# A graph layer with a mixture of experts on one core: which engine does the last addition of the result

## The reference

```python
z   = layernorm(x)
agg = adj @ z + beta[:, None] * z
x   = x + (agg / (adj.sum(1) + beta)[:, None]) @ gnn_kernel + gnn_bias

z      = layernorm(x)
logits = z @ Wr + br                       # 64 experts
gates  = softmax(top_2(logits))            # two per token
y_e    = relu(z @ W1[e] + b1[e]) @ W2[e] + b2[e]
x      = x + gates[:, 0] * y_first + gates[:, 1] * y_second
```

## Time and profile before

| | us |
|---|---|
| median of three runs | 410.21 |
| lowest, highest | 409.86, 410.55 |
| profiled execution | 412.09 |
| its span, first to last instruction | 410.2 |

### The profile page before, as it was taken

How to read it: one execution, slowest core, us unless ns; L and a number is a source line. 1 busy time by engine, 2 the same in 40 slices (tenths; PEclk the granted TensorE clock), 3 DMA queues, 4 the chain that set the end, 5 groups by cost and what they waited for, 6 DMA issues and landing times.

```text
span 410.2 us, 8191 instructions
## 1 busy us (share of the span) xinstructions
PE 347.5 (85%) x1973; PEld 278.4 (68%) x1973; DVE 304.0 (74%) x886; ACT 171.1 (42%) x264; POOL 225.8 (55%) x220
## 2 busy tenths in 40 slices
PE   6989899989999999999999364598999999999200
PEld 2445786876868868688686131498999999999200
DVE  4778689889799898998988262366776767777167
ACT  3485466745855658557480310011111111112063
POOL 3450002058878668576683726075777777777600
PEclk9999899999999999999999758599999999999755
DMA  8999998998978969889680104598999999996097
GB/s 312 369 423 381 347 401 335 389 427 338 419 294 348 408 244 420 325 331 415 241 343 7 47 7 150 165 279 259 300 310 292 295 294 291 295 274 211 27 352 262
DMA packets 45623, 119.25 MB, mean 291 GB/s; under 512 B 7705, under 2 KB 19630, under 8 KB 37410
## 3 DMA queue, kind: packets, MB, share of 16 engines
q1 hardware_dynamic: 27938, 95.88, 62.7%
q10 hardware_dynamic: 12672, 14.58, 11.8%
q0 software_dynamic: 4992, 8.54, 5.7%
HBM read 104.02 MB, written 16.78 MB: 294 GB/s over the span
## 4 chain that ended last, share of the span: by engine, by line
PE 34%; DVE 30%; DMA 16%; ACT 11%; issue 4%; SPq 2%; POOL 2%; POOLq 1%; ACTq 0%; DVEq 0%
DVE adj_low L679 15%; PE bank L978 9%; DMA adj_ring<-adj_t 7%; ACT adj_high L557 6%; PE bank L988 5%; PE bank_pair L988 5%; ACT payload L572 3%; DMA x_sb<-x 3%; PE bank L972 2%; PE bank_pair L985 2%; DMA adj_ring<-dispatched_rows 2%; PE bank L985 2%; PE bank L914 2%; DVE x_sb L842 2%; DMA expert_answers<-adj_ring,ans 2%
## 5 line engine op out<-in xcount | busy, mean ns | idle before, releaser
L679 DVE TENSOR_TENSOR adj_low<-adj_ring,adj_high 128x2048 fp32r<-128x2048 f32 x51 | 116.0, 2286 | 18.5 <-ACT adj_high L557 18.2
L557 ACT CAST adj_high<-adj_ring 128x2048 fp32r<-128x2048 f32 x51 | 97.1, 1905 | 57.7 <-DMA adj_ring<-adj_t 31.9
L502 POOL DMA_INDIRECT dispatched_rows<-payload,slot x64 | 95.2, 1487 | 44.2 <-issue 17.5
L515 POOL DMA_INDIRECT expert_answers<-adj_ring,ans x92 | 90.6, 985 | 43.0 <-ACT adj_ring L610 24.4
L910 PE MATMUL bank<-adj_high,z_hi 128*128 128x512 f32 x204 | 85.0, 417 | 0.9 <-ACT adj_high L557 0.9
L911 PE MATMUL bank<-adj_high,z_lo 128*128 128x512 f32 x204 | 80.2, 393 | 0.0
L821 DVE TENSOR_SCALAR adj_ring<-bank,adj_ring 128x128 f32<-128x128 f32 x184 | 56.0, 346 | 11.9 <-PE bank L978 10.1
L978 PE MATMUL bank<-xt_sb,adj_ring 128*128 128x128 f32 x368 | 57.0, 278 | 0.0
L914 PE MATMUL bank<-adj_low,z_hi 128*128 128x512 f32 x204 | 55.0, 391 | 0.2 <-DVE adj_low L679 0.2
L900 PE MATMUL bank<-adj_ring,z_sb 128*128 128x512 f32 x104 | 48.5, 615 | 3.2 <-DVE z_sb L665 2.8
L978 PEld LDWEIGHTS bank<-xt_sb,adj_ring 128*128 128x128 f32 x368 | 49.3, 195 | 0.0
(11 more groups left out here) (125 smaller groups left out, 426.1 us busy)
## 6 DMA issues: line engine op xcount, KB each, us to landing
adj_ring<-adj_t SPq DMA_DIRECT2D x64, 1024.0 KB, 8.9
adj_ring<-w_pack SPq DMA_DIRECT2D x48, 257.5 KB
adj_ring<-w_pack ACTq DMA_DIRECT2D x44, 257.5 KB
dispatched_rows<-pad_rows SPq DMA_DIRECT2D x8, 528.0 KB, 10.6
adj_ring<-expert_answers SPq DMA_DIRECT2D x8, 512.0 KB, 6.6
adj_ring<-dispatched_rows SPq DMA_DIRECT2D x48, 66.0 KB
adj_ring<-dispatched_rows ACTq DMA_DIRECT2D x44, 66.0 KB
out<-x_sb SPq DMA_DIRECT2D x8, 256.0 KB, 4.0
```

The costliest lines, as they stand in the source:

```text
L502: pool.indirect_dma_start(rows, bass.IndirectOffsetOnAxis(ap=slot[:, b, t, k:k + 1], axis=0), payload[:, b, t, k, :], None).then_inc(scatt ...
L515: pool.indirect_dma_start(y_tok, bass.IndirectOffsetOnAxis(ap=ans[:, s:s + 1], axis=0), y_sb[:, s, :], None, bounds_check=N * K - 1, oob_i ...
L557: nc.scalar.copy(high[:, m % PARTS], adj_sb[:, slot_of(g, k)]).then_inc(hi_ready, 1)
L679: v.tensor_tensor(low[:, m % PARTS], adj_sb[:, slot_of(g, k)], high[:, m % PARTS].bitcast(F32), ALU.subtract).then_inc(lo_ready, 1)
```

## The change

The vector engine no longer does the tensor_tensor, nor does it wait for its own scalar_tensor_tensors or for `scaled`; the last scalar_tensor_tensor of a piece signals a new semaphore. The Pool, behind its loop of scatters, waits for that semaphore and for `scaled`, adds the piece of 128x512 and signals `o_ready`. Sizes, tiles, DMAs and the order of the pieces stay.

```diff
+        first_added = sem("first_added")
...
         @block.gpsimd
...
+            for c in range(OUT_STEPS):
+                tiles = slice(c * OUT_CH, (c + 1) * OUT_CH)
+                pool.wait_ge(first_added, c + 1)
+                pool.wait_ge(scaled, c + 1)
+                pool.tensor_tensor(x_sb[:, tiles, :], x_sb[:, tiles, :], y_in[:, tiles, 1, :], ALU.add).then_inc(o_ready, 1)
...
         @block.vector
...
                 for t in tiles:
                     last = v.scalar_tensor_tensor(out=x_sb[:, t, :], in0=y_in[:, t, 0, :], scalar=gates[:, t, 0:1],
                                                   in1=x_sb[:, t, :], op0=ALU.mult, op1=ALU.add)
-                own.after(last)
-                dve.wait_ge(scaled, c + 1)
-                xs = x_sb[:, tiles[0]:tiles[-1] + 1, :]
-                v.tensor_tensor(xs, xs, y_in[:, tiles[0]:tiles[-1] + 1, 1, :], ALU.add).then_inc(o_ready, 1)
+                last.then_inc(first_added, 1)
```

## The result

The changed kernel takes 418.44 us, median of five runs (417.83 to 420.19), against 410.55 us for the kernel before (five runs, 409.86 to 411.31): a ratio of 1.0195, 95% interval 1.0167 to 1.0223, or 7.9 us more. The direction was forecast; the size was not. The forecast was +2.7 us, and the result lies above the range's end of 416.3 us. The profiled execution has a span of 418.3 us, 8.1 us more than before.

A forecast was written before the change was run, and what follows sets the result against it. The vector engine was taken to bound the tail's second half at 1.77 us a piece. Alternating with the Pool at 2.07 us ends the last addition 2.7 us later: 410.21 + 2.7 = 412.9 us, range 411.0 to 416.3.

The forecast's parts named there:

- What bounds the tail: Second half of the tail: the vector engine sets the pace at 1.77 us a piece; ScalarE needs 1.28 us.
- this bound: Tail's end without exclusion: DMA throughput limits the stores, last landing 407.7 instead of 409.8, 2.0 us less, 408.2 us.
- The two engines exclude each other, and take turns: In the tail, two-input vector instructions and Pool additions block each other by turns: 2.07 us a piece; chance 0.70.
- the sum: Tail, per piece: 0.16 + 1.27 + 0.07 + 0.57 = 2.07 us instead of 1.77; last addition 2.7 us later.
- the faster rival: In the tail, no exclusion for this form: the Pool follows ScalarE at 1.28 us a piece; 408.2 us, chance 0.12.
- The rival in which the vector engine keeps its turn: In the tail, the Pool waits until the scalar_tensor_tensors end at 403.8, then adds eight pieces; 416.1 us, chance 0.10.
- the late Pool: Before the tail's additions, skipped halves cost 1.2 us each, the Pool arrives at 399; 413 to 415 us, chance 0.03.
- The last step of the sum: At the kernel's end, SyncE's last store follows the last addition as before, with 2.0 us to land.
- the bound of the one term in the sum: Tail's piece length if nothing overlaps: 1.14 + 1.27 + 0.16 = 2.57 us a piece, time 416.4 us.
- The statement that the Pool has nothing to do in the tail: Before the tail's additions, the Pool is there in time: last scatter ends at 388.13 us, skipped halves over by 390.8.

The follow-up runs named there:

- e11: Kernel before, but for the last two pieces ScalarE applies the first answer's gate and the vector engine does two tensor_tensors a piece; ratio 0.9996.
- e4: Changed kernel, but the scalar_tensor_tensor reads its first tensor from PSUM, leaving the first answer out of the result; 414.76 us, ratio 1.0082 against the kernel before.
- e8: Changed kernel, but the Pool does a memset on a dead tile in place of each addition; span 412.4 us in a single execution.
- e1: Kernel before, plus one Pool memset of 128x1, read by nothing, behind the vector engine's last addition; 417.35 us against 411.22, ratio 1.0142.
- e3: Kernel before, but the Pool waits for the last addition's semaphore and executes nothing behind it; 416.0 us, ratio 1.0104.
- e9: Changed kernel with one explicit Pool drain between its last scatter and its first addition; 413.29 us against 411.19 for the kernel before, ratio 1.0045.

## Why the prediction was right and wrong

**What bounds the tail: right.** The vector engine's 1.77 us a piece set the end. In e11's trace the last addition moved 0.9 us with the vector engine's shorter pieces. In e4's it came 12.0 us after the tail's start, the DMA engines were full until then (shares of 0.97 to 1.05), and SyncE was through after 14.6 us, 2.1 us under before, where the prediction had 2.0 for this bound.

**The two engines exclude each other, and take turns: right.** Forecast 2.07 us a piece, measured 2.06 between the Pool's additions; scalar_tensor_tensors of up to 1.39 us, the mean 562 ns ("near 0.6 us"); additions of 1.26 to 1.31 us. That the totals agree to 0.01 us is partly luck, two small errors that cancel: an addition took 1.31 us where the sum had 1.27, and the Pool stood still for 0.75 us between two of them where the sum had 0.80 (0.07 + 0.57 + 0.16). The last addition was forecast 2.7 us later and came 2.56 us later, measured from the tail's start. e4 and e8 show that this is the exclusion: take away one SBUF input or the Pool's reading, and it is gone. The narrow reading of the Trainium skill, Advanced Engine Details and Errata, section VectorE Performance Modes (the fast two-port modes alone), one of the grounds for the faster rival, does not hold here: the scalar_tensor_tensor of 0.34 us took 1.39 us. The rival in which the vector engine keeps its turn did not happen, since the Pool's additions begin at 394.23, with most of the vector instructions still to come; nor did the late Pool, which stood idle 6.68 us before its first addition.

**The last step of the sum failed.** It said: "SyncE's last store follows as before, with 2.0 us to land". The store did follow as before, with 2.0 us. What failed is what was left unsaid, that the store still ends the program. The program ends when the last engine has drained, and the Pool's drain costs 8.2 us, hidden in the kernel before because the Pool's last instruction ended at 388 us. Moving the last addition to the Pool moved the drain's 8.2 us from behind 388 to behind 410 us. The term that was priced at nothing is 418.2 - 412.1 = 6.1 us, and e1, e3 and e9 show it: put the drain at the end without the additions, and the kernel is longer (+6.1 and +4.8 us); clear it early with the additions in place, and the loss falls from 7.9 to 2.1 us. The trace of before held the row (a POOLq drain of 9.8 us); the sum asked who produces the last byte and not what each engine still does after its last instruction. Had the 6.1 us been added to the 2.7, the forecast would have been 419.0 us, beside a median of 418.44: +8.8 us, where the medians differ by 7.9.

**The range.** Its upper end, 416.3 us, was about the bound of the one term in the sum, 416.4 us. The width covered the doubt about the length of a piece, which was small, and no doubt about the end of the program. The statement that the Pool has nothing to do in the tail was the place to look, and it was not quite true: the Pool executes nothing there, but its drain runs until 396.3 us. Work moved to an engine that has finished also moves that engine's end.

## What to carry to other kernels

Before work is moved to the end of an engine that finished early, read that engine's end-of-program rows: what it does after its last instruction is hidden only as long as it finishes early. A Pool that has issued indirect DMAs has such work; either keep the Pool out of the last microseconds, or put a drain where it waits anyway, and long enough ahead that it is over when the Pool is needed (in e9 it was not, by 1.9 us). And an addition shared between the vector engine and the Pool is no sharing if both read two SBUF tensors: the one that comes second waits for the other's whole instruction, and 0.69 us of work saved on the vector engine cost it about 1.05 us of hold (1.39 less 0.34).

## What the runs showed of the hardware that was not expected

- The Pool's drain after indirect DMAs takes 0.082 us for each of them (up to 112, in the small programs) on top of 0.06 us, although all have landed: the memset came 19 to 42 us behind the last of them. An explicit drain clears it, and the closing one is then 0.1 us.
- In the programs with 128 and 156 such DMAs of 128 rows of 512 bytes, the drain is shorter by about 113 of them, and the Pool's issue has one gap of 7.2 us, behind the 113th. Other row sizes and a slower issue were not tried, and the kernel itself shows no such gap.
- A closing drain is issued as soon as the sequencer is there, beside the last instruction still running: its recorded 9.57 us in the changed kernel hold the last addition's 1.26 us.
